# GpSimd holds its weight pieces from the 63rd on until 28 of the 32 sums of x are made

## The chip, the cores and the metric

The kernel runs on one core of one Trainium2 chip. A core has five engines with an instruction queue each: TensorE (PE, matrix products), VectorE (DVE), ScalarE (ACT), GpSimd (POOL) and SyncE (SP, which here only issues DMA transfers). They meet through semaphores. Sixteen DMA engines move data between HBM and the on-chip memory (SBUF); transfers issued by SyncE and by GpSimd go through queues of their own, but through the same sixteen engines. The metric is the device time of one execution, in microseconds (us).

## What is computed

4096 tokens of 1024 values are normalised; from the result `xn` come a gated-attention part `s` (three projections, a running sum along the sequence, an output projection) and a feed-forward part with eight experts that share their weights, of which each token uses two within a capacity of 256:

```python
xn = _layernorm(x, axis=-1)
s = _L0_attn_ref(xn, Wq, bq, Wk, bk, Wv, bv, Wo, bo)   # (phi_q * cumsum(phi_k * v)) * SCALE @ Wo.T + bo
g = _silu(_L0_ffn_ref(xn, router_w, w1, b1, w2, b2))   # gelu(buf @ w1.T + b1) @ w2.T + b2, scattered back
x = x + s * g
```

## The kernel before

**Stages.** A front part (until about 465 us) routes the tokens, makes keys, values and their running sums, and packs the kept tokens into `xnT`. Then the main part multiplies the packed tokens with the up-projection weights (w1, later Wq) and the results with the down-projection weights (w2, later Wo). Both use a seven-product scheme for a 2 by 2 block product: instead of eight block products, seven are made of sums of blocks. This needs sums of blocks of x ("sums of x"), of the hidden values, and of the weights. Each number is carried as two halves of 16 bits, high and low, so that a product of blocks is made of three passes (high x high, high x low, low x high).

**The unit of the main part** is a quad (`quad(k)`): seven products (k,0) to (k,6), each of 12 matmuls of 128x512 (`product`, L2275). Quads 0 and 1 come first, then quads alternate with the down-projection (`down(n)`, L2304, 168 matmuls). Product (k,j) needs weight block j of quad k, split into halves by ScalarE (`high_up`, L1105) and then VectorE (`low_up`, L1680), and for j = 2, 4 and 6 a copy of the running result that ScalarE makes (L1123). Products (1,0), (1,1) and so on also wait until values of quad 0 have left their banks: ScalarE makes a quad's four values in L1185.

**Sums of weights.** 80 units ("pieces") are listed in `UNITS`, two for each quad and four for each down-projection, in the order of their need. For each one GpSimd loads 128 partitions x 4 blocks x 256 values (512 KB, `load_unit`, L837), makes four additions (`up_unit` L849 to L854, `down_unit` L860 to L865) and stores the piece to up_sums or down_sums in HBM (`store_unit`, L843, 512 KB). The first 68 (`in_time`) go through a ring of three buffers in the loop at L881 to L888: turn u makes and stores piece u, waits until piece u - 1 is stored, and loads piece u + 2. The ring lies over the last blocks of the down-projection weights, so ScalarE waits for all 68 stores before it splits block 4 of the first down-projection (L1115, then L1116). The last 12 pieces are made later, between other work of GpSimd that follows TensorE's progress (L907 to L929).

**Sums of x.** 32 of them (`x_sum_product(i)`, L2244) are made by TensorE through identity matrices, four or two matmuls each, in the order X_ORDER; `xsum_done` counts them. ScalarE makes the high half (`high_x_sum`, L1096) and VectorE the low half (L1669). From i = 24 on ScalarE writes over places of `xnT` whose contents SyncE first saves to xraw_dram (L685), so it waits for these stores; between the sums it splits the first weight blocks (from i = 20 on, every second one). TensorE makes quad 0 right behind them.

**SyncE** loads weight blocks and stored sums of blocks through a ring of four (`load_up_op`, L632) and of three (`load_down_op`, L642). The load for ring place a is issued when the block four before it is split. All SyncE transfers stand in one order written out by hand (L679 to L738).

Of the kernel before, what the change touches and what calls it, by code (L numbers as in the profile page):

```python
# [93 lines left out]
def build(nc, x, x_t, w_kv, router, w_up, w_down, b_k, b_v, b_q, b_o, b_1, b_2, out):  # L94
# [13 lines left out]
    with ExitStack() as ctx:  # L108
# [3 lines left out]
        def sem(name):  # L112
            return ctx.enter_context(nc.semaphore(name))
# [72 lines left out]
        late_sums = xnT_rows[:, 8:12, HOLE:2 * HOLE]  # L186


        UNITS = [("up", k, c) for k in range(3) for c in range(2)]
        for n in range(GROUPS):  # L190
            UNITS += [("down", n, c) for c in range(4)]
            UNITS += [("up", k, c) for k in (2 * n + 3, 2 * n + 4) if k < 2 * GROUPS for c in range(2)]

        def stored(eng, units):

            for u in range(3):
                last = [i for i in range(units) if i % 3 == u][-1:]
                for i in last:
                    eng.wait_ge(sum_stored[u], 16 * (i // 3 + 1))
# [142 lines left out]
        xsum_done, xsum_hi, xsum_lo = sem("xsum_done"), sem("xsum_hi"), sem("xsum_lo")  # L342
# [175 lines left out]
        def _(sp):  # L518
# [102 lines left out]
            def load_up_op(a):  # L621
# [7 lines left out]
                if name[0] == "S":  # L629
                    stored(sp, UNITS.index(("up", k, 1)) + 1)  # L630
                src = (up_sums if name[0] == "S" else w_up)[k, :, UP_AT[name], :]
                sp.dma_start(up_at(a), src).then_inc(up_loaded[a % US], 16)  # L632

            def load_down_op(d):
# [4 lines left out]
                if name[0] == "T":  # L639
                    stored(sp, UNITS.index(("down", n, 3)) + 1)  # L640
                src = (down_sums[n] if name[0] == "T" else w_down[n].rearrange("p (b c) n -> p b (c n)", b=4))
# [152 lines left out]
        def _(pool):  # L794
# [36 lines left out]
            def unit_at(u):  # L831
                return late_sums if u >= len(UNITS) - LATE_UNITS else sum_ring[u % 3]

            def load_unit(u):
                kind, n, c = UNITS[u]
                src = w_up[n] if kind == "up" else w_down[n].rearrange("p (b c) n -> p b (c n)", b=4)
                pool.dma_start(unit_at(u), src[:, :, c * (BLOCK // 2):(c + 1) * (BLOCK // 2)]).then_inc(sum_loaded[u % 3], 16)  # L837
# [29 lines left out]
            def make_unit(u):  # L867
                if UNITS[u][0] == "up":
                    up_unit(u)
                else:  # L870
                    down_unit(u)
                store_unit(u)
# [8 lines left out]
            for u in range(in_time):  # L881
                make_unit(u)
                if u + 2 < in_time:
                    if u == 0:
                        pool.wait_ge(kv_summed, 1)
                    else:
                        pool.wait_ge(sum_stored[(u - 1) % 3], 16 * ((u - 1) // 3 + 1))
                    load_unit(u + 2)  # L888

            def save_s(n, sums):  # L890
# [16 lines left out]
            for i, n in enumerate((0, 1, 2, 3, 4, 5, 6, 8)):  # L907
                if n > FFN_GROUPS - 1:
                    save_s(FFN_GROUPS - 1, FIRST_SUMS + LAST_SUMS)
                for p in range(8):  # L910
# [9 lines left out]
                    u = in_time + 2 * i + p // 4  # L920
# [1501 lines left out]
```

## Time and profile before

| | |
|---|---|
| median of 3 runs | 1974.89 us (1971.14 to 1975.51) |
| the profiled execution | 1973.73 us, of which the span of instructions is 1971.7 us |
| TensorE busy | 1926.3 us, 98% of the span |
| VectorE busy | 1324.9 us, 67% |
| ScalarE busy | 707.2 us, 36% |
| GpSimd busy | 502.6 us, 25% |
| mean granted TensorE clock | 0.992 of full speed |
| moved by DMA | 424.70 MB, mean 215 GB/s |

Times in the rows below are microseconds from the start of the span unless they are marked ns. A busy TensorE is read as the bound of a stretch; its idle time, with what ended it, tells what was late. The matmuls are pipelined, so that a row's duration is somewhat longer than the distance to the next row.

### The profile page before, as it was taken

The numbers are of one execution on the slowest core, as the hardware profiler recorded it, in microseconds if no ns is written. First come the engines' busy times: TensorE is split into PE (matmuls) and PEld (weight loads), VectorE is DVE, ScalarE is ACT, GpSimd is POOL, SyncE is SP. The second block draws the span as 40 slices with busy tenths as digits, with TensorE's granted clock in tenths as the row PEclk, the third lists the DMA queues.
The fourth block names the chain that finished last, engine by engine and source line by source line (L and its number), as shares of the span: only waits on it lengthen the run. The fifth ranks groups of instructions, "written<-read, shape, count | busy, mean of one in ns | idle before, by whom it ended". The sixth has DMA issues, their size and how long they took to land.

```text
span 1971.7 us, 26822 instructions
## 1 busy us (share of the span) xinstructions
PE 1926.3 (98%) x9406; PEld 886.4 (45%) x9406; DVE 1324.9 (67%) x2027; ACT 707.2 (36%) x1076; POOL 502.6 (25%) x640
## 2 busy tenths in 40 slices
PE   8989999999899999999999999999999999999996
PEld 3444544444344444444444444444444444444442
DVE  7866677778776776777778786565455565456656
ACT  5232222224634434434435542522212322222322
POOL 0068887887221231231210010210000000000002
PEclk9989999999999999999999999999999999999998
DMA  9598788889998998887876889663333233435535
GB/s 396 203 224 246 244 232 258 265 242 291 336 280 285 263 260 266 265 271 242 276 248 222 279 303 338 173 188 97 107 102 101 81 123 98 121 104 168 176 116 127
DMA packets 213550, 424.70 MB, mean 215 GB/s; under 512 B 50960, under 2 KB 102720, under 8 KB 210880
## 3 DMA queue, kind: packets, MB, share of 16 engines
q1 hardware_dynamic: 170976, 293.15, 46.3%
q0 software_dynamic: 34896, 121.71, 20.7%
q10 hardware_dynamic: 7568, 8.42, 1.4%
q8 instruction: 63, 1.03, 0.2%
q14 instruction: 47, 0.39, 0.1%
HBM read 269.03 MB, written 162.58 MB: 219 GB/s over the span
## 4 chain that ended last, share of the span: by engine, by line
PE 76%; POOL 11%; DMA 10%; issue 2%; DVE 1%; ACT 0%; SPq 0%; DVEq 0%; POOLq 0%; ACTq 0%
PE pair L2304 37%; PE pair L2275 36%; DMA arena<-w_up 3%; DMA arena<-w_down 3%; PE pair L2056 2%; POOL arena L853 1%; POOL arena L851 1%; POOL arena L864 1%; POOL arena L837 1%; POOL arena L854 1%; POOL arena L849 1%; DMA xraw_dram<-xnT 1%; POOL arena L860 1%; POOL arena L862 1%; POOL up_sums L843 1%
## 5 line engine op out<-in xcount | busy, mean ns | idle before, releaser
L2304 PE MATMUL pair<-arena 128*128 128x512 f16 x3360 | 730.2, 379 | 1.1 <-DVE arena L1816 0.5
L2275 PE MATMUL pair<-xnT,arena 128*128 128x512 f16 x2400 | 526.6, 380 | 7.9 <-ACT arena L1185 3.4
L2304 PEld LDWEIGHTS pair<-arena 128*128 128x128 f16 x3360 | 327.8, 98 | 400.3 <-issue 7.2
L2056 PE MATMUL pair<-arena 128*128 128x512 f16 x1728 | 387.7, 383 | 10.7 <-DMA arena<-arena 8.3
L1808 DVE SCALAR_TENSOR_TENSOR arena<-pair,arena 128x1024 f32<-128x1024 f32 x234 | 286.0, 1223 | 150.9 <-PE pair L2304 150.0
L1198 ACT ACTIVATE arena<-arena 128x512 f16<-128x512 f32 x280 | 171.4, 626 | 555.6 <-PE pair L2304 500.8
L2275 PEld LDWEIGHTS pair<-xnT,arena 128*128 128x128 f16 x2400 | 234.8, 98 | 293.3 <-ACT xnT L1123 4.0
L2056 PEld LDWEIGHTS pair<-arena 128*128 128x128 f16 x1728 | 167.5, 99 | 215.6 <-issue 15.3
L2275 PE MATMUL pair<-xnT 128*128 128x512 f16 x960 | 213.7, 379 | 0.0
L1783 DVE SCALAR_TENSOR_TENSOR arena<-arena 128x512 f16<-128x512 f32 x280 | 190.9, 694 | 16.4 <-ACT arena L1198 15.7
L896 POOL DMA_DIRECT2D s_dram<-arena x8 | 6.2, 776 | 596.4 <-DVE arena L1808 596.4
L1123 ACT ACTIVATE xnT<-pair 128x512 f32<-128x512 f32 x120 | 71.2, 593 | 220.7 <-PE pair L2275 220.6
L2275 PEld LDWEIGHTS pair<-xnT 128*128 128x128 f16 x960 | 94.0, 98 | 113.2
L915 POOL DMA_INDIRECT meta_dram<-meta,slot_i x32 | 33.8, 1055 | 362.3 <-PE pair L2304 360.4
L1686 DVE SCALAR_TENSOR_TENSOR arena<-arena 128x1024 f16<-128x1024 f32 x70 | 85.5, 1222 | 27.3 <-ACT arena L1116 27.1
L1185 ACT ACTIVATE arena<-arena,b_c 128x512 f32<-128x512 f32 x96 | 69.2, 721 | 75.0 <-DVE arena L1719 38.7
L1000 ACT ACTIVATE arena<-arena 128x512 f32<-128x512 f32 x36 | 22.7, 629 | 155.3 <-DVE arena L1438 152.0
L1726 DVE TENSOR_TENSOR arena<-xnT,pair 128x512 f32<-128x512 f32 x40 | 27.4, 686 | 75.5 <-PE pair L2275 75.5
L1680 DVE SCALAR_TENSOR_TENSOR arena<-arena 128x512 f16<-128x512 f32 x83 | 59.7, 720 | 23.2 <-ACT arena L1105 22.0
L1116 ACT ACTIVATE arena<-arena 128x1024 f16<-128x1024 f32 x70 | 72.8, 1043 | 0.0
L1730 DVE TENSOR_TENSOR arena<-xnT,pair 128x512 f32<-128x512 f32 x40 | 27.5, 687 | 62.2 <-ACT xnT L1123 62.2
L1007 ACT ACTIVATE arena<-arena 128x512 f16<-128x512 f32 x36 | 22.6, 630 | 115.2 <-DVE arena L1458 115.1
(209 smaller groups left out, 1688.9 us busy)
## 6 DMA issues: line engine op xcount, KB each, us to landing
down_dram<-arena SPq DMA_DIRECT2D x70, 512.0 KB, 6.9
arena<-down_dram SPq DMA_DIRECT2D x70, 512.0 KB, 3.3
up_dram<-arena SPq DMA_DIRECT2D x90, 256.0 KB, 6.3
arena<-up_dram SPq DMA_DIRECT2D x90, 256.0 KB, 2.6
arena<-down_sums SPq DMA_DIRECT2D x40, 512.0 KB
arena<-w_up POOLq DMA_DIRECT2D x36, 512.0 KB, 6.3
up_sums<-arena POOLq DMA_DIRECT2D x36, 512.0 KB, 4.9
arena<-up_sums SPq DMA_DIRECT2D x67, 256.0 KB
```

What stands on the lines that cost most here:

```text
L915: pool.indirect_dma_start(meta_dram, bass.IndirectOffsetOnAxis(ap=slot_i[:, t:t + 1].bitcast(U32), axis=0), meta[:, t, :], None, bounds_ch ...
L1116: nc.scalar.activation(down_ring[:, j, :, HI, :], down_stage[d % DS].rearrange("p (c n) -> p c n", c=2), ACT.Copy, scale=WM).then_inc(down ...
L1123: nc.scalar.activation(dst, in_rows(src), ACT.Copy).then_inc(copy_ready, 1)
L1185: nc.scalar.activation(g_block(name), src, ACT.Gelu, bias=b1_c[:, col:col + 1], scale=INV_XM)\
L1198: nc.scalar.activation(g_ops[:, A_NAMES.index(name), k % 2, HI, :], g_block(name), ACT.Copy, scale=CS if is_attention(n) else HS).then_inc ...
L1680: nc.vector.scalar_tensor_tensor(up_ring(j)[:, LO, :], up_at(a), WM, up_ring(j)[:, HI, :], ALU.mult, ALU.subtract).then_inc(up_w[j], 16)
L1686: nc.vector.scalar_tensor_tensor(down_ring[:, j, :, LO, :], down_stage[d % DS].rearrange("p (c n) -> p c n", c=2), WM, down_ring[:, j, :, ...
L1783: nc.vector.scalar_tensor_tensor(to[:, LO, :], g_block(name), CS if is_attention(k // 2) else HS, to[:, HI, :], ALU.mult, ALU.subtract).th ...
L1808: ins = nc.vector.scalar_tensor_tensor(to, src, scale, to, ALU.mult, ALU.add)
L2056: ins = mm(out_bank(n), xT[u][:, a, c, :], wkv[:, (n // 2) * CH + c, b, e], start=(c == first and i == 0), stop=(c == last and i == 2), sk ...
L2275: ins = mm(out_to, w[:, a, c * P:(c + 1) * P], x_in_op[:, b, c, :], start=(first and i == 0), stop=(i == 11), skip_group_check=True)
L2304: ins = mm(down_banks(j, t // 2)[:, (t % 2) * BLOCK:(t % 2 + 1) * BLOCK], g_ops[:, A_NAMES.index(DOWN_A[j]), c, a, t * P:(t + 1) * P], dow ...
```

## The change

One constant and one wait are added. In the turn u = 60 of the loop over the first 68 pieces, after piece 60 is made and stored and piece 59's store has landed, GpSimd waits until `xsum_done` is 28, and then loads piece 62. All that follows in the loop follows that wait.

```diff
@@ -186,6 +186,7 @@
+        UNITS_BEFORE_SUMS = 62
         UNITS = [("up", k, c) for k in range(3) for c in range(2)]
@@ -885,6 +886,8 @@
                         pool.wait_ge(kv_summed, 1)
                     else:
                         pool.wait_ge(sum_stored[(u - 1) % 3], 16 * ((u - 1) // 3 + 1))
+                    if u + 2 == UNITS_BEFORE_SUMS:
+                        pool.wait_ge(xsum_done, 28)
                     load_unit(u + 2)
```

## Rows read from the trace of the kernel before

**Rows 1.** The page's costliest groups: name, shapes, count | busy us, mean ns | idle before.
```profile
L2304 PE MATMUL pair<-arena 128*128 128x512 f16 x3360 | 730.2, 379 | 1.1 <-DVE arena L1816 0.5
...
L2275 PE MATMUL pair<-xnT,arena 128*128 128x512 f16 x2400 | 526.6, 380 | 7.9 <-ACT arena L1185 3.4
```

**Rows 2.** Timeline of TensorE: start, duration, what, count, idle time before and what ended it.
```profile
491.70 5.34 PE L2275 MATMUL pair<-xnT,arena 128*128 128x512 f16 x24 [1.33 <-DVE xnT L1669]
500.20 7.94 PE L2275 MATMUL pair<-xnT,arena 128*128 128x512 f16 x36 [3.16 <-ACT xnT L1123]
...
519.28 12.04 PE L2275 MATMUL pair<-xnT,arena 128*128 128x512 f16 x48 [3.37 <-ACT arena L1185]
```

**Rows 3.** Stretches of 2 us: length, busy time of each engine, clock, DMA share, GB/s.
```profile
518.00:520.00 2.00, 0.72 (x2) 0.28 (x3) 1.80 (x3) 2.00 (x4) 0.00 (x0) 0.74 0.91 323
520.00:522.00 2.00, 2.00 (x6) 0.73 (x5) 1.73 (x2) 1.17 (x3) 0.00 (x0) 0.50 1.01 360
```

**Rows 4.** Timeline of ScalarE: landings that it waited for, and the value for TensorE.
```profile
490.23 0.60 ACT L1096 ACTIVATE xnT<-pair 128x512 f16<-128x512 f32 x1 [4.38 <-DMA xraw_dram<-xnT]
...
499.03 0.63 ACT L1105 ACTIVATE xnT<-arena 128x512 f16<-128x512 f32 x1 [0.95 <-DMA arena<-up_sums]
...
514.83 0.63 ACT L1105 ACTIVATE arena<-spare 128x512 f16<-128x512 f32 x1 [3.44 <-DMA spare<-up_sums]
...
518.56 0.67 ACT L1185 ACTIVATE arena<-pair,b_c 128x512 f32<-128x512 f32 x1
```

**Rows 5.** Long stretches: length, PE, PEld, DVE, ACT, POOL busy, clock, DMA share, GB/s.
```profile
465.00:487.00 22.00, 22.00 (x115) 10.47 (x114) 20.12 (x35) 14.81 (x29) 14.18 (x20) 1.00 1.01 356
487.00:513.00 26.00, 21.10 (x97) 9.11 (x96) 17.11 (x25) 13.81 (x24) 17.15 (x22) 1.00 0.98 295
513.00:534.00 21.00, 17.63 (x76) 7.51 (x75) 16.13 (x24) 14.22 (x24) 0.07 (x1) 0.92 0.91 336
```

**Rows 6.** Timeline of GpSimd: store of piece 60, load of 62, store of 67.
```profile
463.44 0.74 POOL L843 DMA_DIRECT2D up_sums<-arena  x1 [0.30 <-POOL arena L854]
465.70 0.78 POOL L837 DMA_DIRECT2D arena<-w_down  x1 [1.52 <-DMA up_sums<-arena]
...
512.33 0.73 POOL L843 DMA_DIRECT2D up_sums<-arena  x1 [1.01 <-POOL arena L854]
```

**Rows 7.** Timeline of TensorE: the matmuls that end sum of x 27.
```profile
486.60 1.03 PE L2244 MATMUL pair<-xnT,ident 128*128 128x512 f16 x4
```

**Rows 8.** Timeline of ScalarE, block 4; and the longest wait, 455 to 600.
```profile
550.11 1.05 ACT L1116 ACTIVATE arena<-arena 128x1024 f16<-128x1024 f32 x1
...
POOL meta_dram L915 <- PE pair L2304: 54.0, 3, 47.8
```

**Rows 9.** Timeline of SyncE's issues, and GpSimd's loads (L837) to landing.
```profile
492.18 0.32 SPq L632 DMA_DIRECT2D arena<-up_sums  x1
...
503.23 0.75 SPq L632 DMA_DIRECT2D spare<-up_sums  x1
...
DMA to landing us min/median/max: 4.0/6.6/12.7
```

**Rows 10.** VectorE's L1680: one instance; then min/median/max ns to 515, and after.
```profile
487.88 1.22 DVE L1680 SCALAR_TENSOR_TENSOR arena<-arena 128x512 f16<-128x512 f32 x1
...
L1680 DVE SCALAR_TENSOR_TENSOR arena<-arena x8: 681/692/1223, 484.1 to 508.9; 128x512 f16<-128x512 f32 x8
L1680 DVE SCALAR_TENSOR_TENSOR arena<-spare,arena x1: 925/925/925, 501.4 to 501.4; 128x512 f16<-128x512 f32 x1
...
L1680 DVE SCALAR_TENSOR_TENSOR arena<-arena x4: 685/690/693, 527.7 to 534.5; 128x512 f16<-128x512 f32 x4
```

**Rows 11.** Timeline: first and last of eleven of VectorE's, ScalarE's copy behind it.
```profile
518.51 0.68 DVE L1680 SCALAR_TENSOR_TENSOR xnT<-arena,xnT 128x512 f16<-128x512 f32 x1
...
525.88 0.68 DVE L1719 TENSOR_TENSOR arena<-xnT,pair 128x512 f32<-128x512 f32 x1
...
527.22 0.58 ACT L1123 ACTIVATE xnT<-pair 128x512 f32<-128x512 f32 x1
```

## The prediction

> **What bounds the kernel now.** I read the costliest groups first, for TensorE's idle time: L2275, the products of x with the up-projection weights, stands still for 7.9 us, and L2304, the down-projection that alternates with it to the end, for 1.1 us [rows 1]. The timeline of TensorE places the 7.9: 1.33 us before 491.70, 3.16 us before 500.20 and 3.37 us before 519.28, all in the first two quads of products, right behind the sums of x [rows 2]. As so little idle time follows, a microsecond won or lost there reaches the end of the program undiminished. A second cost lies beside the last gap: from 518 to 520 the granted clock is 0.74 and from 520 to 522 it is 0.50, the lower of the two levels, after TensorE had stood idle [rows 3]. That is (1 - 0.74) x 2 + (1 - 0.50) x 2 = 1.5 us of work. So 7.9 + 1.5 = 9.4 us is all there is to win.
>
> ScalarE's waits name what ends the gaps. It waited 4.38 us for the store of x to xraw_dram before 490.23, 0.95 us for a weight load at 499.03 (its copy right behind it released TensorE at 500.20), and 3.44 us for one at 514.83; behind that load it had queued the value (518.56 to 519.23) that released TensorE at 519.28 [rows 4]. All three are landings. The DMA engines are full: share 1.01 from 465 to 487 at 356 GB/s, 0.98 from 487 to 513 at 295 GB/s, and still 0.91 from 513 to 534, where GpSimd was busy for 0.07 us [rows 5]. GpSimd's weight pieces (512 KB in, 512 KB out, each) are a good part of the first two stretches, and nothing waits for them soon.
>
> **What the change does in time.** It stands in turn u = 60 of the loop over 68 pieces: piece 60 is stored at 463.44, and load 62, now at 465.70 [rows 6], waits until 28 of the 32 sums of x are made. The 28th is i = 27, whose two matmuls are the first half of the x4 group at 486.60; it is done near 487.1 [rows 7]. So the wait lasts about 487.1 - 465.7 = 21.4 us. Queued behind it on GpSimd is not load 62 alone but the making of piece 61, already loaded: seven pieces are made after it. One piece takes (512.33 - 465.70) / 7 = 6.7 us now, so the last store moves from 512.33 [rows 6] to about 487.1 + 4 (piece 61) + 6 x 6.7 = 531. Its first consumer is ScalarE before the fifth down-projection block, which lies over the ring of pieces: L1116 at 550.11 [rows 8]. Some 12 us of cover after the landing, so no cost; without it every microsecond would be TensorE's. GpSimd's next own work waited 54.0 us for TensorE in this region and has the 20 us too [rows 8].
>
> **What it frees.** Four loads and three stores (7 x 0.524 = 3.67 MB) leave the stretch up to 487: at 356 GB/s 10.3 us of full DMA engines [rows 5]. The store of x then lands near 481, before ScalarE can use it: i = 24 is made some six matmuls of 0.22 us before 486.60, near 485.3. The 4.38 us wait is gone. What is late next is VectorE. Its split at 487.88 (1.22 us) is held by its own queue [rows 10]; two sums and a split later, 3 x 0.65 us, the third weight block is ready at 491.0. Now that releases the load issued at 492.18, which ScalarE has at 499.03, 6.85 us on [rows 4, 9]; it goes 1.2 us earlier. GpSimd's loads of twice its size landed in 4.0 us at the fastest [rows 9], so it lands between 1.2 us (no relief) and 1.2 + 2.85 = 4.0 us earlier. I take 2.5, the middle, off the second gap; TensorE, with 24 matmuls of its own from 490.1, could use 4.9.
>
> **What it gives back at the next gate.** The load that ends the third gap is issued at 503.23, behind three down-projection loads, and ScalarE has it 11.6 us later [rows 4, 9]. It will be issued 2 us earlier (4 at best), following the second gap. But GpSimd's traffic is denser there: two pieces in 13.5 us (2.1 MB) against the rest of store 65, load 67 and store 66 (1.6 MB): 0.5 MB more, at 295 GB/s 1.7 us; the bounds are 0 (GpSimd alone is slowed) and 2.4 us. So the gain at 519.28 lies between 2 - 2.4 = -0.4 and +4 us. I take **1.5 us**, a little under the middle, because the bytes speak for the low end and only the emptier queue at 487 for the high one. The gap itself gets longer, as TensorE comes to it earlier, and the clock's 1.5 us stays.
>
> **What it adds after 513.** GpSimd was silent here and now makes two to three pieces. First, DMA: some 2 MB more at 336 GB/s [rows 5] is 6 us at the very worst, spread over loads with a few us of cover. Second, VectorE: the split L1680 takes 0.685 to 0.693 us after 515; before, where GpSimd's additions run beside it, up to 1.223 us, and 0.925 us at 501.4; the one at 487.88 is the longest [rows 10]. From 518.51 to 526.5 VectorE runs eleven operations almost back to back, ten on two SBUF inputs and then the sum at 525.88, and ScalarE's copy at 527.22 (end 527.80) hangs on it [rows 11]. TensorE's product (1,4), the last 12 of the 48 matmuls from 519.28, starts near 519.28 + 12.04 - 7.94 / 3 = 528.6 [rows 2]: cover 0.8 us. An operation is lengthened by 0 (most of the eight early ones, median 0.692) to 0.54 (the longest), 0.24 by the single row; at 0.2, 10 x 0.2 - 0.8 = **1.2 us** of stall, bounds 0 and 10 x 0.54 - 0.8 = 4.6. Late loads fall in the same places and are not added.
>
> The Trainium skill ("SBUF — State Buffer", section "🔬 SBUF: two separate sides") has a rule that speaks against this change: VectorE's operations with two SBUF inputs and GpSimd's contend for one port pair by an exclusive lock, and the loser blocks for the whole instruction. The stretched splits before 515 and none after agree with it [rows 10]; by the rule taken to its end, the sum would be that of the slower rival below.
>
> **The sum.** 1973.73 us (profiled execution: span 1971.7 and 2.0 around it) - 1.5 + 1.2 = 1973.4 us. The median of the runs lies 1.16 us above that execution, so the forecast for the median is 1974.6 us. This is no change: 0.2% (3.95 us) is about what a measurement of this kernel can tell from none.
>
> **The rivals.** *Faster, the gates stay open:* the second gate opens 4.0 us earlier, the load of 503.23 goes out and lands 4.0 us earlier, since GpSimd's queue is the one that is slowed; the third gap no longer drops the clock (1.5 us), and VectorE's delays stay within their cover. 1974.89 - 5.5 = 1969.4 us. For it: the waits are landings just behind GpSimd's traffic [rows 4]. Against: the bytes are only moved by 20 us, into engines that are 0.98 and 0.91 full [rows 5]. *Slower, GpSimd under VectorE:* the additions of pieces 64 to 67 fall on the ten operations ahead of (1,4). It decides from a total delay of 0.8 us on; at the worst row's 0.54 us each it is 4.6 us, with nothing won at 519.28: 1979.5 us. For it: the small cover, and the rows of 0.925 and 1.223 us [rows 10]. Against: the median of 0.692 us beside a GpSimd that was busy for 17.15 of 26 us [rows 5, 10]. *It does nothing:* the wait would already be met when reached, 1974.9 us. The rows exclude it, 465.70 against 487.
>
> **How the numbers follow.** The forecast (within 0.2%) has 0.53, the faster case 0.26, the slower one 0.21; the one that does nothing gives the forecast's time and is counted there. The forecast's own range is 1970.9 to 1978.8. To leave out no more than 2 in 10 the range reaches to the faster rival and nearly a microsecond past it, 1968.5, and half a microsecond past the slower one, 1980.0. Faster 0.26, same 0.53, slower 0.21.
>
> **What would show it.** Right: ScalarE's wait for xraw_dram gone; GpSimd idle from 464 to 487 and busy to about 531; a second gap of about 1 us, a third longer than 3.37 us that still ends in a weight load, with the clock at its lower level behind it; L1680 and its like longer than 0.69 us between 515 and 531, and a new gap of TensorE near 528. Wrong: that weight load landing 3 us or more before 514.8 and the clock staying at 1.00; or new gaps of over 4 us in the second quad; or GpSimd ending after 545.

## The result: slower by 0.2%, and where the profile of the changed kernel puts it

| | kernel before | changed kernel |
|---|---|---|
| median of 12 runs | 1972.43 us | 1974.76 us |
| ratio, 95% interval | | 1.0020 (1.0011 to 1.0029) |
| profiled execution | 1973.73 us | 1979.41 us |
| its span | 1971.7 us | 1977.2 us |

The ratio stands for 3.9 us (2.2 to 5.7). It is no ratio of the two medians, which differ by only 2.3 us, so the size of the loss is less sure than that it is one. One run of the kernel before took 8034.89 us; it is left out of the ratio. The forecast was 1974.6 us with 0.21 on slower: the median lies inside the range, but the sum gave a gain of 0.3 us, and the whole interval of the ratio lies on the slower side.

A line of the changed kernel's file is 3 higher than in the kernel before behind the edit (L2275 is now L2278, L1185 is L1188, L1123 is L1126), 1 higher ahead of it (L837 is L838). First the timeline of TensorE in the changed kernel, the rows that answer to [rows 2]:

```profile
492.75 0.59 PE L2247 MATMUL pair<-xnT,ident 128*128 128x512 f16 x2
493.18 13.14 PE L2278 MATMUL pair<-xnT,arena 128*128 128x512 f16 x60
506.16 5.34 PE L2278 MATMUL pair<-xnT 128*128 128x512 f16 x24
511.34 2.75 PE L2278 MATMUL pair<-xnT,arena 128*128 128x512 f16 x12
518.06 10.49 PE L2278 MATMUL pair<-xnT,arena 128*128 128x512 f16 x36 [3.97 <-ACT arena L1188]
529.53 2.76 PE L2278 MATMUL pair<-xnT,arena 128*128 128x512 f16 x12 [0.98 <-ACT xnT L1126]
...
542.71 12.22 PE L2278 MATMUL pair<-xnT,arena 128*128 128x512 f16 x48 [2.64 <-ACT arena L1188]
```

The first two gaps of [rows 2] are gone altogether: quad 0 runs without a stop from 493.18. The third, before (1,1), is 3.97 us. Two are new: 0.98 us before (1,4), and 2.64 us before (2,1). The stretches that answer to [rows 5]; the last three columns are the clock, the DMA share and GB/s:

```profile
465.00:487.00 22.00, 22.00 (x116) 10.47 (x114) 18.20 (x32) 14.07 (x27) 0.00 (x0) 1.00 0.75 247
487.00:513.00 26.00, 26.00 (x122) 11.71 (x121) 19.58 (x31) 15.63 (x28) 16.52 (x19) 1.00 0.75 257
513.00:534.00 21.00, 16.05 (x63) 6.46 (x61) 19.69 (x23) 13.13 (x22) 16.60 (x16) 0.84 1.02 385
```

Up to 487 GpSimd does nothing and the DMA engines are at 0.75 instead of 1.01; from 513 to 534, where they had 0.91 with GpSimd silent, they are full, and the granted clock of that stretch is 0.84 instead of 0.92. GpSimd's timeline answers to [rows 6]: load 62, and the last store.

```profile
491.33 0.78 POOL L838 DMA_DIRECT2D arena<-w_down  x1 [29.93 <-PE pair L2247]
...
541.28 0.74 POOL L844 DMA_DIRECT2D up_sums<-arena  x1 [1.01 <-POOL arena L855]
```

One profile is not enough for a difference of 0.2%: TensorE came to the first sum of x at 464.6 us in the kernel before and at 468.1 in the changed one, over instructions that the change doesn't touch, and in all the profiles below that time lies between 462.2 and 467.2. So I compare three parts by TensorE's timeline: from the first sum of x (L2244) to the first product, from there to the first down-projection (L2304), and the rest.

| kernel | sums of x | quads 0, 1, 2 | both | rest |
|---|---|---|---|---|
| before, first and second profile | 27.1, 26.4 | 62.8, 58.2 | 90.0, 84.6 | 1417.2, 1417.2 |
| changed, first and second profile | 25.1, 25.1 | 66.8, 65.5 | 91.8, 90.6 | 1417.3, 1417.2 |

The rest is equal within 0.1 us. The sums of x gain 1.3 to 2.1 us and the quads lose 3.9 and 7.3; the net is +1.8 us in the first pair of profiles and +6.0 in the second. That their mean, 3.9, is the ratio's figure is in part luck: the kernel before alone differs by 5.4 us from one profile to the other. So a stretch of 85 to 92 us from a single profile, as each experiment below has one, weighs less than the ratio of its runs. "The stretch" below is the column "both", "the rest" the last column.

### The profile page after: what moved, and what is told of

The parts are those of the page before. It is cut to its first block, busy times and chain, and to the rows that moved or that the text cites. A ratio compares the mean times of both kernels' runs of the same rounds, so it can differ in the third digit from the quotient of the medians.

```text
span 1977.2 us, 26823 instructions
## 1 busy us (share of the span) xinstructions
PE 1930.0 (98%) x9406; PEld 887.2 (45%) x9406; DVE 1340.0 (68%) x2027; ACT 708.3 (36%) x1076; POOL 512.2 (26%) x640
## 3 DMA queue, kind: packets, MB, share of 16 engines
q8 instruction: 63, 1.03, 0.2%
## 4 chain that ended last, share of the span: by engine, by line
PE 92%; DMA 4%; DVE 2%; issue 1%; ACT 0%; POOL 0%; SPq 0%; ACTq 0%; DVEq 0%; POOLq 0%
PE pair L2307 37%; PE pair L2278 35%; PE pair L2059 17%; DMA arena<-arena 2%; PE pair L2247 1%; DMA xnT<-w_kv 1%; PE pair L2172 1%; PE pair L2051 1%; PE pair L2019 1%; DMA spare<-up_sums 1%; DMA arena<-up_sums 0%; PE pair L2038 0%; DVE xnT L1672 0%; DVE arena L1683 0%; POOL out L940 0%
## 5 line engine op out<-in xcount | busy, mean ns | idle before, releaser
L2278 PE MATMUL pair<-xnT,arena 128*128 128x512 f16 x2400 | 529.5, 381 | 7.6 <-ACT arena L1188 6.6
L1201 ACT ACTIVATE arena<-arena 128x512 f16<-128x512 f32 x280 | 171.5, 626 | 558.4 <-PE pair L2307 500.8
L2278 PEld LDWEIGHTS pair<-xnT,arena 128*128 128x128 f16 x2400 | 235.4, 98 | 295.2 <-ACT arena L1188 7.6
L2278 PE MATMUL pair<-xnT 128*128 128x512 f16 x960 | 213.7, 379 | 0.0
L1126 ACT ACTIVATE xnT<-pair 128x512 f32<-128x512 f32 x120 | 71.2, 593 | 221.5 <-PE pair L2278 221.4
L2278 PEld LDWEIGHTS pair<-xnT 128*128 128x128 f16 x960 | 93.9, 98 | 113.3
L1188 ACT ACTIVATE arena<-arena,b_c 128x512 f32<-128x512 f32 x96 | 69.2, 721 | 77.8 <-DVE arena L1722 39.6
L1729 DVE TENSOR_TENSOR arena<-xnT,pair 128x512 f32<-128x512 f32 x40 | 27.4, 685 | 76.9 <-PE pair L2278 76.9
L1733 DVE TENSOR_TENSOR arena<-xnT,pair 128x512 f32<-128x512 f32 x40 | 27.4, 686 | 62.2 <-ACT xnT L1126 62.2
L1722 DVE TENSOR_TENSOR arena<-xnT,pair 128x512 f32<-128x512 f32 x40 | 27.4, 684 | 53.9 <-PE pair L2278 53.3
```

Of the source, the lines that this page charges most:

```text
L1126: nc.scalar.activation(dst, in_rows(src), ACT.Copy).then_inc(copy_ready, 1)
L1188: nc.scalar.activation(g_block(name), src, ACT.Gelu, bias=b1_c[:, col:col + 1], scale=INV_XM)\
L1201: nc.scalar.activation(g_ops[:, A_NAMES.index(name), k % 2, HI, :], g_block(name), ACT.Copy, scale=CS if is_attention(n) else HS).then_inc ...
L2278: ins = mm(out_to, w[:, a, c * P:(c + 1) * P], x_in_op[:, b, c, :], start=(first and i == 0), stop=(i == 11), skip_group_check=True)
```

## The experiments

Two theories of the loss stood against each other. **T**: the held transfers, now in quads 0, 1 and 2, make weight loads land late. **P**: the held additions of GpSimd slow VectorE's operations there. **C**, beside them: the idle time costs twice, by the lower clock behind it. The core of each edit is shown; all other lines are those of the kernel named. Where a ratio is given, it is against the kernel before.

### Profiles again

Both kernels, profiled a second time.

> The kernel before, profiled again, to see what of its gaps and of its stretch repeats. By the first profile: gaps of 1.3, 3.2 and 3.4 us, the stretch from the first sum of x to the first down-projection 89.9 us. If the profile on record was one of its slower executions (1973.7 us, where the medians of its runs were 1972.4 and 1969.8), the stretch or the front part before it is shorter here by 1 to 4 us.

> The changed kernel, profiled again. By its first profile: first two gaps gone, third 4.0 us, new ones of 1.0 us before (1,4) and 2.6 us before (2,1), stretch 91.8 us. If the loss of 0.2% is made in this stretch, it is 2 to 5 us longer than that of the kernel before in its second profile, and the part behind it is equal within 0.3 us (1417.2).

The kernel before, second profile, TensorE:

```profile
491.32 5.34 PE L2275 MATMUL pair<-xnT,arena 128*128 128x512 f16 x24 [1.13 <-DVE xnT L1669]
497.71 5.34 PE L2275 MATMUL pair<-xnT,arena 128*128 128x512 f16 x24 [1.05 <-ACT xnT L1123]
505.51 2.76 PE L2275 MATMUL pair<-xnT,arena 128*128 128x512 f16 x12 [2.46 <-ACT xnT L1123]
508.11 5.34 PE L2275 MATMUL pair<-xnT 128*128 128x512 f16 x24
513.29 13.11 PE L2275 MATMUL pair<-xnT,arena 128*128 128x512 f16 x60
```

Gaps of 4.6 us instead of 7.9, all in quad 0, and none before (1,1): TensorE runs from 505.51 on, and the clock is 1.00 from 513 to 534. So what I took for the kernel's third gap and its clock drop is not in each execution. And the DMA engines have no room in that stretch, though GpSimd does nothing there:

```profile
513.00:534.00 21.00, 21.00 (x99) 9.48 (x97) 18.43 (x28) 16.78 (x29) 0.00 (x0) 1.00 0.99 359
```

The share of 0.91 in [rows 5] comes of a hole while TensorE stood still: the share was 0.36 from 516 to 518 and 0.97 from 518 to 534. The changed kernel repeats better: 4.61 us before (1,1), 1.51 before (1,4), 0.94 before (1,6), 1.11 before (2,1), 0.63 before (2,4), 8.8 us in all.

### The additions away

The changed kernel, with the additions of pieces 61 to 67 made on one column, so that those sums of weights are left unmade:

```diff
-                w11, w12, w22, w21 = (unit_at(u)[:, b, :] for b in range(4))
+                w11, w12, w22, w21 = (unit_at(u)[:, b, 0:1 if 61 <= u < 68 else BLOCK // 2] for b in range(4))
```

> The changed kernel, with the four additions of each of the held pieces 61 to 67 made on one column instead of 256 (those sums of weights are left unmade); loads, stores and waits stay. Theory P (the held additions slow VectorE through quads 0 and 1): the operations on two SBUF inputs fall back to 0.69 us there, the gap before product (1,4) (0.98 us) goes, and the stretch from the first sum of x to the first down-projection, 91.8 us with the change and 90.0 before, falls to about 88 to 89. Theory T (the held transfers delay the weight loads): the gaps stay within 1 us of the changed kernel's, 7.6 us in all, and the stretch stays at 91 to 92.

Ratio 1.0023 (1.0013 to 1.0033), stretch 90.2 us: no faster than the changed kernel. VectorE's operations of 512 values are all back at 0.64 to 0.69 us and the gap before (1,4) is gone, but the one before (1,1) is 5.45 us, behind a weight load:

```profile
510.18 0.63 ACT L1108 ACTIVATE arena<-spare 128x512 f16<-128x512 f32 x1 [5.69 <-DMA spare<-up_sums]
```

That speaks for T, with a flaw: relieved of its additions, GpSimd ran ahead (last store at 521.16 instead of 541.28), so its transfers fell denser on quads 0 and 1.

### The additions alone

The kernel before, with additions on data that nothing uses, behind the 32nd sum of x:

```diff
...
+            for products in (8, 9, 11, 13):
+                pool.wait_ge(up_done, products)
+                for b in range(4):
+                    w = late_sums[:, b, :]
+                    extra.link(nc.gpsimd.tensor_tensor(w, late_sums[:, (b + 1) % 4, :], w, ALU.add))
```

> The kernel before, with 16 additions of 128x256 added on GpSimd, four after each of the products (1,0), (1,1), (1,3) and (1,5), on data that nothing uses, and no transfer added. Theory P: VectorE's operations beside them take up to 1.2 us instead of 0.69, TensorE gets a new gap before (1,4) or (2,1) of 1 us or more in all, and the stretch grows from 90.0 to about 91 to 92.5. Theory T: no new gap over 0.3 us, 90.0 to 90.3.

Ratio 1.0029 (1.0015 to 1.0043), stretch 92.1 us. GpSimd made twelve of the sixteen additions back to back from 512.67 to 527.10; TensorE and VectorE beside them:

```profile
527.20 4.77 PE L2283 MATMUL pair<-xnT,arena 128*128 128x512 f16 x12 [5.12 <-ACT xnT L1131]
```

```profile
515.64 1.74 DVE L1694 SCALAR_TENSOR_TENSOR arena<-arena 128x1024 f16<-128x1024 f32 x1
517.30 1.21 DVE L1688 SCALAR_TENSOR_TENSOR xnT<-arena,xnT 128x512 f16<-128x512 f32 x1
518.43 1.21 DVE L1772 TENSOR_TENSOR arena<-arena 128x512 f32<-128x512 f32 x1
...
525.24 0.67 DVE L1727 TENSOR_TENSOR arena<-xnT,pair 128x512 f32<-128x512 f32 x1
```

From 513.37 to 525.24 each operation on two SBUF inputs takes 0.42 to 0.53 us more (1.10 to 1.21 for 0.68, 1.74 for 1.22), the one with an input in PSUM (`pair`) nothing. The row of operations ahead of (1,4) is the one of [rows 11], and the gap before (1,4) is 5.12 us where I had given 4.6 as the upper bound. (A gap of 1.62 us before (1,1) began at 512.52, ahead of the additions.) So P is a real mechanism, and under additions back to back nearly each operation pays the worst row of [rows 10]. In the changed kernel the additions come four at a time with pauses, and were not run alone as they lie there. The Trainium skill ("SBUF — State Buffer", "🔬 SBUF: two separate sides") describes it as an exclusive lock between GpSimd and VectorE operations with two SBUF inputs; the trace agrees on which operations are hit and which not.

### The transfers alone

The kernel before, with four loads and four stores of 512 KB (the last store, behind the loop, isn't shown):

```diff
...
+            for t, products in enumerate((8, 9, 11, 13)):
+                pool.wait_ge(up_done, products)
+                if t:
+                    pool.dma_start(scratch[t - 1], late_sums).then_inc(extra, 16)
+                    pool.wait_ge(extra, 32 * t)
+                pool.dma_start(late_sums, w_up[t, :, :, 0:BLOCK // 2]).then_inc(extra, 16)
+                pool.wait_ge(extra, 32 * t + 16)
```

> The kernel before, with four loads and four stores of 512 KB added on GpSimd's queue in quads 1 and 2, paced by the products (1,0), (1,1), (1,3) and (1,5), and no addition. It is the transfers alone, as the kernel with 16 additions was the additions alone (stretch 92.2, VectorE's operations 1.21 instead of 0.68 us, a gap of 5.12 us). Theory T: weight loads land late in quads 1 and 2, TensorE has new gaps of 1 us or more, the stretch grows by 1 to 3 us to 91 to 93. Theory P: VectorE's times stay 0.68, the late landings stay within their cover, the stretch is 90 to 90.5.

Ratio 1.0034 (1.0024 to 1.0044); one of the nine runs took 2048.28 us and is left out of it. VectorE stays at 0.64 to 0.69 us. There are gaps of 2.17 us before (1,1), 0.63 before (1,4), 2.27 before (2,1) and 0.63 before (2,4). They stand where the changed kernel has gaps, but the first is no effect of the edit: it began at 517.13, and the first added load was issued behind it.

```profile
517.74 0.78 POOL L911 DMA_DIRECT2D xnT<-w_up  x1 [10.22 <-PE pair L2287]
519.30 7.94 PE L2287 MATMUL pair<-xnT,arena 128*128 128x512 f16 x36 [2.17 <-ACT arena L1197]
```

The stretch is 90.0 us, as in the first profile of the kernel before, which is what P was expected to give. Those added transfers whose landing GpSimd waited for took 5 to 9 us each, the eighth was issued at 574.04 only, the later pieces were pushed back, and TensorE had a gap of 3.31 us at 613.15: the rest grew by 6.4 us, and that is nearly all of the 6.7 us that the ratio stands for. So the experiment shows that eight transfers cannot be put there for nothing; of what they cost in quads 1 and 2 it shows nothing.

### The additions away, the transfers kept in time

The changed kernel, additions on one column as above (those sums are left unmade), and:

```diff
+            PACE = {62: 2, 63: 4, 64: 8, 65: 9, 66: 11, 67: 14}
             for u in range(in_time):
+                if u in PACE:
+                    pool.wait_ge(up_done, PACE[u])
                 make_unit(u)
```

> The changed kernel with the additions of the held pieces on one column (those sums are left unmade), and now the pieces kept to the times that they have in the changed kernel: pieces 62 to 67 are made and stored after products (0,1), (0,3), (1,0), (1,1), (1,3) and (1,6). Without that pacing GpSimd ran ahead (last store at 521 instead of 541 us) and its transfers fell denser on the loads of quads 0 and 1. Theory T (transfers alone explain the loss): late weight loads at the same places, stretch 89.5 to 92, ratio 1.0015 to 1.0035. Theory P (the additions under VectorE are the larger part once the transfers are no denser than in the changed kernel): gaps of at most 3 us in all, the clock up, stretch 84 to 87.5, ratio 0.9985 to 1.0005.

Ratio 1.0023 (1.0011 to 1.0036), stretch 90.2 us. The last store is at 539.71 (541.28 in the changed kernel), those before it 3 to 7 us earlier than there. TensorE, with gaps before (1,1), (1,4) and (1,6), and ScalarE's loads behind the first and the last of them:

```profile
515.24 7.94 PE L2281 MATMUL pair<-xnT,arena 128*128 128x512 f16 x36 [2.62 <-ACT arena L1191]
523.80 2.76 PE L2281 MATMUL pair<-xnT,arena 128*128 128x512 f16 x12 [0.62 <-ACT xnT L1129]
...
532.86 4.22 PE L2281 MATMUL pair<-xnT 128*128 128x512 f16 x12 [3.70 <-ACT xnT L1129]
```

```profile
510.79 0.63 ACT L1111 ACTIVATE arena<-spare 128x512 f16<-128x512 f32 x1 [3.77 <-DMA spare<-up_sums]
...
531.69 0.63 ACT L1111 ACTIVATE arena<-arena 128x512 f16<-128x512 f32 x1 [5.19 <-DMA arena<-up_sums]
```

VectorE is at 0.64 to 0.70 us throughout quads 1 and 2, and the time is as long. GpSimd's running ahead is mostly gone, and T stands: with the held transfers and without the held additions the loss has the changed kernel's size.

### The order of SyncE's loads

The changed kernel, with:

```diff
+            save_up(1, (0,))
             for d in range(DS):
                 load_down_op(d)
-            save_up(1, range(5))
+            save_up(1, range(1, 5))
```

> The changed kernel, with SyncE's load of weight block (1,4) and its turn of saves put ahead of the three down-projection loads instead of behind them; nothing else. In the changed kernel's two profiles that load's landing ends the third gap (4.0 and 4.6 us), and the clock falls behind it. Theory G (the gap moved from the first two gates to this one, behind 1.5 MB in SyncE's own queue): the third gap falls under 1 us, the clock stays up, the stretch falls from 91.8 and 90.7 to 85 to 88, the time to about that of before or 1 to 2 us below. Theory D (total bytes decide, whatever their order): a gap of 3 us or more stays, perhaps before another product, and the time stays within 1 us of the changed kernel's.

Ratio 1.0017 (1.0007 to 1.0027), stretch 88.7 us. The gap before (1,1) fell to 1.83 us, and in its place stand 3.33 us before (1,4) and 1.66 before (2,4). The load was the gate of (1,1), but moving it up gained nothing that the ratio shows. This alone doesn't prove that the bytes decide (theory D of the expectation), as the gap before (1,4) has P's mark too: VectorE's operations ahead of it took up to 1.21 us, and 1.74 for 1.22.

Both edits together, SyncE's order and the additions on one column:

> The changed kernel with both single edits together: SyncE's load of block (1,4) ahead of the three down-projection loads, and the additions of the held pieces 61 to 67 made on one column instead of 256 (those sums are left unmade). Each alone left the time where it was (ratios 1.0017 and 1.0023, stretches 88.7 and 90.2): with the load early, gaps of 3.3 and 1.7 us stood before (1,4) and (2,4), where VectorE's operations are stretched; with the additions gone, the third gap was 5.5 us. If these are two separate causes that take over from each other, both together clear most of it: no gap over 1.5 us, stretch 82 to 86, time equal to or below before by up to 4 us. If the transfers alone are enough whatever the order, a gap of 3 us or more stays and the stretch is 88 or more.

Ratio 1.0035 (1.002 to 1.005), stretch 90.4 us: gaps of 0.83 us in quad 0, 2.82 before (1,1), now behind the load of another block (ScalarE waits 3.97 us for `arena<-w_up` at 512.83), 0.92 before (1,6) and 2.28 before (2,1). The expectation asked for a gap of 3 us or more, and the largest is a little under it. The DMA engines are at 1.03 and 415 GB/s from 513 to 534. GpSimd ran ahead here too (last store at 525.90). The transfers are enough in either of the two orders.

### The clock

The changed kernel, with 16 matmuls into a bank that is free, ahead of the wait of product (1,1):

```diff
+                if k == 1:
+                    for _ in range(16):
+                        mm(out_bank(4), ident[:, :], x_op("11")[:, 0, 0, :], start=True, stop=True)
```

> The changed kernel, with 16 matmuls added on TensorE right before the wait of product (1,1), 3.5 us of work whose result nothing uses, in a gap of 3.97 us. Theory C (the gap costs a second time, by the lower clock behind it): the granted clock stays at 1.00 from 518 to 534, where it is 0.84 over 513 to 534 now, and the stretch falls by 1.5 to 3 us, to 89 to 90.3. If the clock costs nothing because TensorE then waits for VectorE and loads anyway, the clock stays up but the stretch stays at 91.5 to 92.

Ratio 1.0023 (1.0012 to 1.0035), stretch 90.5 us. Of the gap before (1,1) 1.09 us are left, and the clock stays at 1.00 over it, up to 522. But TensorE then stands 3.25 us before (1,4), and the lower level comes behind that gap instead:

```profile
520.00:522.00 2.00, 0.73 (x4) 0.12 (x2) 2.00 (x4) 1.91 (x5) 0.51 (x1) 1.00 1.03 390
522.00:524.00 2.00, 0.02 (x1) 0.02 (x2) 2.00 (x4) 1.87 (x5) 1.78 (x2) 0.69 1.04 411
524.00:526.00 2.00, 2.00 (x5) 0.72 (x6) 2.00 (x3) 1.48 (x3) 1.96 (x2) 0.50 1.01 411
```

Keeping the clock at one gap moved the idle time to the next, and nothing was won. The lower clock is a part of the loss, but it comes with the idle time, and filling one gap did not take it away. That a faster TensorE then waits for the same loads and the same VectorE is argued from the gap before (1,4).

### Half of the hold

The changed kernel, holding from piece 65 on:

```diff
-        UNITS_BEFORE_SUMS = 62
+        UNITS_BEFORE_SUMS = 65
```

> The changed kernel with the hold at piece 65 instead of 62: half of the transfers and additions are held, pieces 62 to 64 are loaded early as before. If loss goes with what falls into quad 1, GpSimd ends at about 520 to 525 instead of 541, no addition reaches the products before (2,4), the gap before (2,1) goes, and the stretch is 86 to 89 us; the time is within 1.5 us of before. If the hold itself costs (the emptier queue ahead of 487 is worth nothing, the burst behind it is what hurts), it is as slow as the changed kernel, stretch 90 to 92.

Ratio 1.0006 (0.9996 to 1.0016), stretch 86.4 us, last store at 515.27 us. Gaps of 1.66 us in quad 0 and 3.34 before (1,1), none behind it. With half of the pieces held, and nothing of them in quad 1 past 520, what is lost is within the noise. This fits a loss that goes with what falls into quads 1 and 2, and speaks against one that lies in the hold itself. It halves transfers and additions together, so it doesn't tell them apart.

### The pieces moved out of quads 0 and 1

The kernel before, with pieces 62 to 67 made among the later ones:

```diff
-        LATE_UNITS = 12
+        LATE_UNITS = 18
...
-                    u = in_time + 2 * i + p // 4
+                    u = in_time + 3 * i + (0, 0, 1, 1, 1, 2, 2, 2)[p]
                     if u < len(UNITS):
-                        if p % 4 == 0:
+                        if p in (0, 2, 5):
...
-                        elif p % 4 == 2:
+                        elif p in (1, 4, 7):
```

> The kernel before, with pieces 62 to 67 taken out of the loop altogether and made with the later ones, behind xsum_done 32 and between the first down-projections, three pieces to each of six down-projections instead of two. Nothing of them lies in quads 0 and 1. If the change's gain (first gaps of 1.33 and 3.16 us gone) is real and its loss is only where the pieces were put, the stretch falls to 84 to 87 us and the kernel is faster than before by 3 to 6 us (1967 to 1970). If instead the gain is eaten by the third gap whatever GpSimd does, the stretch is 88 to 90 and the time within 2 us of before.

Ratio 1.0007 (0.9997 to 1.0016). The stretch is 80.3 us, 4 to 10 us shorter than in the kernel before and shorter than I expected, with one gap of 0.63 us; the clock is 1.00. But the kernel is not the 3 to 6 us faster that I expected: the rest is 1424.9 us instead of 1417.2. TensorE stood 2.10, 2.14, 1.00 and 1.56 us before the fifth product of quads 4, 6, 8 and 10, where VectorE's row of operations has its small cover.

The same six pieces, with all three of a down-projection made ahead of its seventh product:

```diff
+                    u = in_time + 3 * i + p // 2
+                    if p < 6 and u < len(UNITS):
+                        if p % 2 == 0:
...
+                        else:
```

> As the kernel with pieces 62 to 67 made among the later ones, three to a down-projection, but each of the three is made ahead of the seventh product of its down-projection (loads after products 1, 3 and 5, additions after 2, 4 and 6), so that no addition runs into the following quad, where that kernel's TensorE had gaps of 2.10, 2.14, 1.00 and 1.56 us. Theory P: those gaps go, the part behind the first down-projection falls from 1424.9 to 1417 to 1418 us, the stretch of quads stays at 80 to 82, and the time is 1960 to 1964 us where before has 1970, ratio 0.995 to 0.997. If it is not the additions but three pieces' transfers in a down-projection that cost, the gaps stay and the part behind stays above 1422.

Ratio 0.9992 (0.9982 to 1.0001), stretch 79.9, rest 1422.3. The gaps shrank to 1.10 us each but stayed. By my expectation that spoke for the transfers, but the trace shows that the edit had not done what it was for. The row of TensorE, VectorE's operations ahead of it, and GpSimd's:

```profile
609.92 2.76 PE L2275 MATMUL pair<-xnT,arena 128*128 128x512 f16 x12 [1.10 <-ACT xnT L1123]
```

```profile
602.43 1.21 DVE L1680 SCALAR_TENSOR_TENSOR xnT<-arena,xnT 128x512 f16<-128x512 f32 x1
603.56 1.21 DVE L1764 TENSOR_TENSOR arena<-arena 128x512 f32<-128x512 f32 x1
604.80 0.69 DVE L1768 TENSOR_TENSOR arena<-arena 128x512 f32<-128x512 f32 x1
```

```profile
601.50 1.59 POOL L864 TENSOR_TENSOR xnT<-xnT 128x256 f32<-128x256 f32 x1
603.05 1.17 POOL L865 TENSOR_TENSOR xnT<-xnT 128x256 f32<-128x256 f32 x1
```

The third piece was late, since the second took 23 us through the one buffer that they share (569.72 to 593.09, of it 13 until its load was there, 3 of additions, 7 of store), and the third's additions fell from 599.44 to 604.22 on the operations ahead of (4,4). As they end, VectorE is back at 0.69. So I moved that piece's additions behind (k,4), and kept piece 62 in the ring:

```diff
-        LATE_UNITS = 12
+        LATE_UNITS = 17
...
+                        else:
+                            if p == 5:
+                                pool.wait_ge(up_done, 7 * (2 * n + 4) + 5)
```

> The kernel before with pieces 63 to 67 made among the later ones, three pieces to a down-projection, the third one's additions held until product (k,4) of the even quad behind it is done. In the kernel with 18 late pieces VectorE's operations took 1.21 instead of 0.68 us at the end of quad 3 and the start of quad 4, beside that third piece (599.4 to 604.2), and TensorE stood 1.10 us before (4,4), (6,4), (8,4) and (10,4). Theory P: with the additions out of that row those four gaps go, the part behind the first down-projection is 1417.2 to 1418 us, the stretch 80 to 83, the span 1961 to 1965, ratio 0.996 to 0.998. If the gaps came of the transfers, they stay at 1 us each and the part behind at 1421 or more.

Ratio 0.9964 (0.9951 to 0.9978), median 1964.56 us where the kernel before had 1971.16 on the same chip: 6.6 us faster. Stretch 80.5, rest 1418.3, span 1962.8. Of the four gaps one of 0.36 us is left. TensorE's groups from 489 us to the end:

```profile
L2306 PE MATMUL pair<-arena 128*128 128x512 f16 x3360 | 730.2, 379 | 1.1 <-DVE arena L1818 0.5
L2277 PE MATMUL pair<-xnT,arena 128*128 128x512 f16 x2400 | 525.4, 379 | 1.1 <-ACT xnT L1125 1.0
```

The 7.9 us of L2275 in [rows 1] are 1.1 here. So P is shown at this place as far as such an edit can: the third piece's load stayed ahead of the row, and with the additions behind it VectorE takes 0.68 to 0.69 us in it. Its store moved along with the additions, and one piece fewer is made late.

## Why the prediction was wrong

**What bounds the kernel: right in mechanism, wrong as a size.** The gaps are landings, and nothing after them is regained: the rest agrees within 0.1 us. But "9.4 us is all there is to win" was read off one execution. The second holds less: there the gaps are 4.6 us, there is none before (1,1), and the clock stays at 1.00. The gain of 1.5 us at (1,1) came out so: from the last sum of x to (1,1) TensorE took 29.1 us in the first profile of before (490.2 to 519.28) and 25.9 in the second (to 515.88); in the changed kernel 24.9 and 25.5. That is 3.6 to 4.2 us won against the profile on record, about the prediction's upper bound of 4, and 0.4 to 1.0 against the second. A forecast for a median cannot add a gain to an execution whose gaps are above the usual.

**What the change does in time: right.** The wait bites; I put load 62 at 487.1 and it came at 491.33, of which 3.6 us are the later start of this execution. The last store was late by 10 us (541.28 for 531): 4.2 from load 62, the rest because the seven pieces took (541.28 - 491.33) / 7 = 7.1 us each, the first one 4.9 and the six behind it 7.5, instead of 4 and 6.7. The cover ahead of block 4 held.

**What it frees: right, and more than I gave.** ScalarE's wait for xraw_dram is gone, and the second gap went wholly, 3.16 us where I took 2.5.

**What it gives back, and what it adds after 513: the step that failed.** I put the loss there at 1.2 us, all VectorE's, and wrote of the transfers that they were "spread over loads with a few us of cover" and, as late loads, "not added". From the start of (1,1) to the first down-projection the kernel before took 35.3 and 33.7 us, the changed one 41.9 and 40.0: a loss of 6.5 us in the mean. Some 3.9 of them are idle time of TensorE (3.62 and 4.19 us behind (1,1), none in the kernel before), and the other 2.6 are the lower clock behind the gaps. So the failed step is the term for late loads, which I put at nothing because they would "fall in the same places". The kernel with the additions away and the transfers in time has a loss of the same size with VectorE unhindered. The bytes were too few as well: from load 65 (511.88) on the changed kernel has three loads and four stores, 3.7 MB and not 2, which at 385 GB/s is 9.5 us of full DMA engines. And the cover of "a few us" had no row under it. The average of 0.91 in [rows 5] hid that the engines are full wherever TensorE runs: at 0.99, with GpSimd silent, in the second profile.

**VectorE: right mechanism, wrong price, and not the term that decides.** The gap that the 1.2 us stood for, before (1,4), measured 0.98 and 1.51 us, behind a (1,1) at the lower clock that gave VectorE more time. That is near by luck, as the price was wrong: in quad 1 of the changed kernel an operation beside an addition mostly paid 0.42 to 0.53 us, not 0.2. The median of 0.692 us in [rows 10] misled me: GpSimd's 16 additions fill only 12.9 of those 26 us. In the trace of the kernel before, of the eleven L1680 operations up to 515, the five that lie beside no addition took 0.68 to 0.69 us, and the six beside one 0.70, 0.90, 0.93, 0.99, 1.14 and 1.22.

With the additions away the loss stays (1.0023 against 1.0020), so they add nothing on top of the transfers that the ratio can tell. My reading is that the two hold up the same products, so that the later one counts. The other half of it is not shown: the changed kernel was not run with its additions and without its transfers. The 1.0029 of the additions alone can't be set beside these two: there they stood in the kernel before, closer together, and without what the hold gains.

**The rivals.** The slower one named the right side and nearly the right loss (4.6 us, the ratio's being 3.9), but by the additions; its time of 1979.5 us lies 4.7 above the median. That the transfers alone would do it was no rival of mine. The faster one asked for gates that stay open, and the version with the pieces moved out has them: stretch 80.5 us.

## What to carry to other kernels

Work that is held back from a crowded stretch is worth what the next stretch can take: ask there for the cover of the transfers that share its DMA engines, not only for free time on the holding engine. Moving pieces 62 to 67 by 20 to 30 us lost 0.2%; moving 63 to 67 by 80 us and more, into the down-projections and clear of VectorE's tight row, won 0.36% (0.22 to 0.49). And an average share of the DMA engines over a stretch in which the main engine stood still says little of the room there: look at the parts in which it runs. Last, before a gain is taken from the gaps of one profile, profile the kernel again: here the idle time to be won was 7.9 us in one execution and 4.6 in the next.

## What the runs showed of the hardware that I had not expected

Beside additions of GpSimd on 128x256 made back to back, a VectorE operation on two SBUF inputs is mostly longer by 0.52 to 0.53 us, on 512 values (0.68 to 1.21) and on 1024 (1.22 to 1.74) alike; where it lies beside them only in part, values between occur (0.81 to 1.18), and once it was 1.45. One with an input in PSUM stays at 0.67. Under the same overlap GpSimd's additions mostly take 1.05 to 1.59 us instead of 0.72.

How long TensorE stood does not tell by itself whether the clock falls behind it. A gap of 3.97 us was followed by about 5 us at the lower level (0.50 from 517 to 523), and one of 2.64 us in the same execution by some 3 us of it (0.50 from 544 to 546). One of 3.16 us in the first profile of the kernel before, and one of 2.46 us in its second, were followed by none.
